# Second attention layer: output bias as a row of WO, image part added on TensorE in the head transposes, norms folded into the context columns, small steps in other slots

## The reference

```
q, k_t, v_t = heads(x @ W_q), heads(text @ W_k), heads(text @ W_v)
probs_t  = softmax(q k_t^T * scale)
text_out = probs_t v_t
k_ip, v_ip = heads(ip @ W_k_ip), heads(ip @ W_v_ip)
qsem     = l2norm(probs_t @ text)                 # per head, over 512 channels
sem      = qsem . l2norm(ip)                      # per head, 4 values
probs_ip = softmax(q k_ip^T * scale + 0.5 * sem) * spatial_mask
out = (text_out + probs_ip v_ip) @ W_out + b_out + x
```

## Time and profile before

| | |
|---|---|
| median of 3 runs | 1884.32 us |
| lowest, highest | 1880.2, 1893.85 us |
| the profiled execution | 1886.43 us |
| its span, first to last instruction | 1883.9 us |
| mean granted TensorE clock | 0.937 |
| PE busy | 1698.1 us (90%) |
| DVE busy | 1458.5 us (77%) |
| ACT busy | 1037.1 us (55%) |
| POOL busy | 876.7 us (47%) |

### The profile page before, as it was taken

The page is one execution under the profiler, slowest core; times in us unless marked ns, Lnnn a source line. Parts: engine busy times, 40 slices in busy tenths (PEclk is TensorE's granted clock), DMA queues, the critical chain, the costliest instruction groups (busy, mean ns, idle before and its releaser), DMA issues.

```text
span 1883.9 us, 42199 instructions
## 1 busy us (share of the span) xinstructions
PE 1698.1 (90%) x14344; PEld 1480.7 (79%) x14344; DVE 1458.5 (77%) x3732; ACT 1037.1 (55%) x2188; POOL 876.7 (47%) x714
## 2 busy tenths in 40 slices
PE   5999999999999998479998989898899989889885
PEld 4888888888888886368787878788788878878764
DVE  4677777777777777448988888888888888888884
ACT  3466666666666665236655555555455655545551
POOL 4223233323333321445664665566466656646563
PEclk9899999999999999679998999989898999989997
DMA  6333444434434432533233223313322331332210
GB/s 170 94 112 115 122 118 121 122 114 120 120 117 117 122 94 63 155 93 91 65 90 81 76 69 85 89 42 90 80 76 65 91 88 46 86 81 69 60 34 21
DMA packets 186492, 172.65 MB, mean 92 GB/s; under 512 B 25884, under 2 KB 186282, under 8 KB 186282
## 3 DMA queue, kind: packets, MB, share of 16 engines
q1 hardware_dynamic: 186282, 169.97, 32.1%
HBM read 110.19 MB, written 57.59 MB: 89 GB/s over the span
## 4 chain that ended last, share of the span: by engine, by line
PE 26%; DVE 15%; POOL 8%; issue 7%; ACT 2%; SPq 1%; DMA 0%; DVEq 0%; ACTq 0%; POOLq 0%
PE MISC L60 9%; PE GP L60 6%; DVE PM L1077 4%; DVE ZP L1071 4%; POOL NRM L1242 3%; PE PV L787 3%; PE NAT L736 3%; POOL ZS L1221 3%; DVE MX L1063 2%; PE TR L757 2%; PE PV L790 1%; POOL XTSL L1249 1%; ACT P L933 1%; PE MISC L886 1%; DVE NRM L1096 1%
## 5 line engine op out<-in xcount | busy, mean ns | idle before, releaser
L1221 POOL TENSOR_TENSOR ZS<-ZP 128x256 f32<-128x256 f32 x320 | 312.2, 978 | 392.5 <-DVE ZP L1071 392.1
L314 ACT ACTIVATE P<-TA 128x512 f32<-128x512 f32 x320 | 202.2, 633 | 253.5 <-DVE TA L460 252.8
L60 PE MATMUL GP<-PH,GH 128*128 128x256 f32 (+1 forms) x960 | 263.8, 302 | 50.9 <-DVE ZP L1071 50.1
L1077 DVE SCALAR_TENSOR_TENSOR PM<-P,PH 128x512 f32<-128x512 f32 x320 | 279.7, 874 | 0.0
L1071 DVE TENSOR_TENSOR ZP<-GP,PM 128x512 f32<-128x512 f32 x320 | 219.7, 687 | 70.4 <-PE GP L60 57.7
L60 PE MATMUL GP<-PH,GL 128*128 128x256 f32 (+1 forms) x960 | 254.6, 292 | 0.0
L1063 DVE TENSOR_REDUCE MX<-NAT 128x2 f32<-128x504 f32 x320 | 215.9, 676 | 40.1 <-PE NAT L736 38.0
L60 PEld LDWEIGHTS GP<-PH,GH 128*128 128x128 f32 (+1 forms) x960 | 191.9, 200 | 66.6 <-issue 41.1
L445 DVE TENSOR_REDUCE MX<-NAT 128x2 f32<-128x154 f32 x320 | 101.8, 318 | 172.2 <-PE NAT L142 170.2
L933 ACT ACTIVATE P<-TR 128x512 f32<-128x512 f32 x320 | 189.8, 593 | 63.5 <-PE TR L757 58.0
L460 DVE TENSOR_TENSOR TA<-TR,ST 128x512 f32<-128x512 f32 x320 | 219.1, 686 | 3.0 <-PE TR L162 2.8
...
## 6 DMA issues: line engine op xcount, KB each, us to landing
...
```

The lines of the kernel that those rows point to most:

```text
L60: ins = e.matmul(out, lhs, rhs, start=(n == 0), stop=(n == len(pairs) - 1))
L314: e.activation(P[:, s % NP, :], TA[:, s % 2, :], ACT.Exp, scale=SCALE).then_inc(q["exp"], 1)
L1077: e.scalar_tensor_tensor(PM[:, s % 2, :], P[:, s % NP, :], 2.0, PH[:, s % NS, :].bitcast(F32), ALU.mult, ALU.subtract).then_inc(q["pm"], 1)
L1221: e.tensor_tensor(ZS[:, s % NZ, :], ZP[:, s % 2, 0:S], ZP[:, s % 2, S:2 * S], ALU.add).then_inc(q["zs"], 1)
```

## The change

Both layers:

- The output bias is no longer added to the residual XB by POOL. WO gets it as row 111 of its third chunk, and HS a column C of ones; the chunks of the heads start at CO = (0, 112, 209).

Second layer:

- `ipm` and DVE's two additions of the image part are gone. The head transposes are now ordinary matmuls of HS with the identity, and a second matmul, VIP with PT, accumulates the image part into the same bank. `hst` is split over two slots.
- The factor 0.5 / norm of the image tokens is multiplied into the four image columns of CT by DVE (`ctn`, slot -8) before the context is split into CTSH and CTSL, so the multiplication by RN in FU goes. The norm step moves from ONCE = -12 to NORM = -34, and its input is loaded earlier.
- The norm of qsem: a product, a maximum and a scaled product become one scalar_tensor_tensor.
- The mask is applied in F1 (two scalar_tensor_tensor) and not to FM. SC is scaled by ACT and has three buffers.
- GL, HTL and the output addition stand one slot after the PE step they read, ahead of MX. Other small steps get other slots.

```diff
-    AT = dict(q=(-3, 1, 5), k=(-2, 2, 6), spill=(-1, 3, 7), x_in=-22, xts=-12, c_in=-18, cts=-6, gr=(4, 8), v=(10, 12), kbd=12, scm=14,
-              vip_in=20, vip=32, cmb=46, root=(46, 47, 48, 49), sem=(52, 53, 54), fu=55, tx=(56, 57, 58), ptt=59, ipm=61, hst=64, om=(69, 73), out=75,
-              xb_in=59, xb=63)
-    ONCE = -12
+    AT = dict(q=(-3, 1, 5), k=(-2, 2, 6), spill=(-1, 3, 7), x_in=-22, xts=-12, c_in=-18, ctn=-8, cts=-6, gr=(4, 8), gl=(5, 9), v=(10, 12), kbd=11, scm=14,
+              vip_in=34, vip=44, cmb=47, root=(47, 48, 49, 50), inv=53, f0=55, f2=57, sub=58, sum=60, f1=61, ptt=63, tx=63, hst=(67, 71),
+              htl=(68, 72), om=(75, 78), y=(76, 79), out=80, xb_in=63)
+    ONCE, NORM = -12, -34
...
-            b = due(t, AT["ipm"])
-            if b is not None:
-                for i in range(2):
-                    k, free = ring.take(("ipm", b, i), (q["hs"], 2 * b + i + 1))
...
-                    e.matmul(k[:, 0:C], PT[:, i * 128:(i + 1) * 128], VIP[:, b % 2, :], start=True, stop=True).then_inc(q["ipm"], 1)
...
+            for i, off in enumerate(AT["hst"]):
+                b = due(t, off)
+                if b is not None:
                     k, free = ring.take(("hst", b, i), (q["ht_lo"], 2 * b + i + 1))
                     e.wait_ge(*free)
                     if i == 0:
...
-                    for c, c0 in enumerate(CC):
-                        ins = e.transpose(k[0:CK, c * 128:(c + 1) * 128], HS[:, i, c0:c0 + CK], IDENT[:, :])
+                        e.wait_ge(q["tx"], b + 1)
+                        e.wait_ge(q["pt"], b + 1)
+                        e.wait_ge(q["vip"], b + 1)
+                    for c, c0 in enumerate(CO):
+                        e.matmul(k[0:CK, c * 128:(c + 1) * 128], HS[:, i, c0:c0 + CK], IDENT[:, :], start=True, stop=False)
+                        ins = e.matmul(k[0:CK, c * 128:(c + 1) * 128], VIP[:, b % 2, c0:c0 + CK], PT[:, i * 128:(i + 1) * 128], start=False, stop=True)
...
+            if t == NORM:
                 k, free = ring.take("rnm", (q["rn"], 1))
-                e.wait_ge(*free)
+                if free:
+                    e.wait_ge(*free)
                 e.wait_ge(q["once_q"], 1)
                 e.wait_ge(q["fill"], FILLS)
...
+            for n, off in enumerate(AT["gl"]):
+                b = due(t, off)
+                if b is not None:
...
+            for i, off in enumerate(AT["htl"]):
+                b = due(t, off)
+                if b is not None:
...
+            for i, off in enumerate(AT["y"]):
+                b = due(t, off)
+                if b is not None:
...
+            b = due(t, AT["inv"])
             if b is not None:
                 e.wait_ge(q["nrm"], 4 * b + 4)
...
+                e.scalar_tensor_tensor(NRM[:, 2, :, :], heads_of(b)[:, :, :, D], EPS, NRM[:, 1, :, :], ALU.mult, ALU.max).then_inc(q["cmb"], 1)
+                e.wait_ge(q["cmb"], 4 * b + 3)
                 e.reciprocal(NRM[:, 3, :, :], NRM[:, 2, :, :]).then_inc(q["cmb"], 1)
...
+            b = due(t, AT["ctn"])
+            if b is not None:
+                if b == 0:
+                    e.wait_ge(q["rn"], 3)
+                e.wait_ge(q["c_in"], 16 * (b + 1))
+                e.tensor_tensor(CT[:, :, NT:T], CT[:, :, NT:T], RN[:, 1, NI * b:NI * b + NI].unsqueeze(1).broadcast_to([128, KC, NI]),
+                                ALU.mult).then_inc(q["ctn"], 1)
+            if t == NORM:
+                e.wait_ge(q["norm"], 1)
                 e.tensor_copy(RN[:, 0, :], ring.bank["rnm"][:, 0:NIP]).then_inc(q["rn"], 1)
...
-            b = due(t, AT["xb"])
-            if b is not None:
-                e.wait_ge(q["xn_in"], 16 * (b + 1))
-                e.tensor_tensor(XB[:, :, :], XB[:, :, :], BIAS[:, :].unsqueeze(1).broadcast_to([128, 2, C]), ALU.add).then_inc(q["xb"], 1)
```

234 lines of the change are left out of this document (100 added, 134 removed).

## The result

The changed kernel takes 1777.74 us (median of 4, 1777.2 to 1785.6) against 1882.26 us before on the same chip (median of 4): a ratio of 0.9445, 95% interval 0.9395 to 0.9495. The forecast was 1806, with a range from 1784 to 1853. So the sign was right, and the time lies 6 us outside the range, on the fast side. The profiled execution took 1777.3 us, its span is 1775.2 us.

The account below looks back on a forecast made before the run. PE was taken as near its bound in the second layer, losing time to waits and half clock. 1886.4 - 78 - 4 + 1 + 4 - 2 = 1807, run median 2 lower, so 1805; stated 1806, range 1784 to 1853.

Parts of the forecast that it names:

- The bound and the slot rule: Second layer: PE near its bound; a slot costs the larger of 1.2 us + PE's extra and 1.93 + DVE's extra.
- PE's added work: Steady batch of the second layer: PE's own work rises by 0.9 us, to 54.2 us.
- The half clock: Steady batch: 1.5 us counted for one spell at 1.2 GHz in slots 15 or 16.
- The row of 13 batches: Second layer, steady batches: each gains 6.2 us, taken as 6.0, so 13 of them give 78 us.
- rival C: Second layer: no half clock at all, 57.5 us a batch or less, 1782 us in all; chance 0.10.
- Slots 3 and 4: Steady batch: slot 3 falls to 4.0 us without the bias addition, slot 4 from 6.3 to 2.3, the largest gain.
- GL's move: Slot 4: GL one slot on, counted with the absent transposes as the largest gain, 6.3 us now to 2.3.
- Slots 12 to 14: Steady batch: these slots take 2.7, 2.6 and 2.3 us, against 5.0, 3.2 and 5.2 before.
- PM in slots 3, 7 and 15: PM multiply on DVE: 1.83 us in slot 3, about 1.8 in slot 7, 2 or more in slot 15.
- The start: Second layer's start: first K 20 us late, near 812.3, but net loss only 4 us; bounds 0 and 16.
- The first layer: Bias addition leaving POOL gains 0 us there, since PE is the bound with only 1% idle.
- The end: From the last square root to the span's end: net gain 2 us, bounds 0 and 4.

## Why the prediction was right or wrong

**The bound and the slot rule: right.** The new slots, predicted and measured: 0 to 3: 2.7, 2.4, 2.3 to 2.6, 4.0 against 2.39, 2.70, 2.15, 3.65; 4 to 7: 2.3, 2.3, 2.6, 4.4 against 2.37, 2.40, 2.59, 4.53; 8 to 11: 2.3, 1.9, 3.0, 4.4 against 2.11, 1.93, 2.96, 4.53; 12 to 15: 2.7, 2.6, 2.3, 4.1 against 3.05, 2.82, 2.11, 4.35; 16 to 19: 1.9, 2.7, 3.95, 2.7 against 1.93, 2.91, 3.70, 2.83. The sum is 58.0 measured and 57.5 + 0.5 predicted. That it fits so closely is partly luck: single slots miss by up to 0.35 and cancel. Slot 3 came out 0.35 shorter, 0.26 of it by the HS multiply, which takes 0.74 up to the start of the next instruction where the forecast had 1.0; slot 12 came out 0.35 longer, since PM still takes 1.86 in it, beside two ZS in a row. (The forecast read the 2.00 of PM in slot 12 as beside CTSL; CTSL starts only in slot 14.) PE's added work was 1.0 against 0.9, though its whole, 54.2 forecast against 56.0 by busy time, was 1.8 short, as that of before was.

**The half clock: the step that failed.** The sum held 1.5 us a batch "for one half-clock spell in slots 15 or 16". Measured is one spell of 3.4 us in twelve batches, and that batch took 59.2 us against 58.0, so 0.1 us a batch. The term was 1.4 too large, 18 us over 13 batches. The row of 13 batches was missed by 18.6: 19.5 for the whole term of 1.5, 2.6 for rounding 6.2 down to 6.0 and 1.9 for slots a little shorter, less 5.4 the other way, because the mean of these batches before was 65.4 and not 65.8 (batch 14, near the end, took 60.8). The mechanism of rival C decided, with a chance of 0.10, and C's 1782 is 4 us off. The evidence that I set against C was one stretch of before, PE busy 2.44 of 3.40 us and half clock behind it. It was a stretch of a kernel that lost 5.9 us a batch in other places too, and I carried it over to one that loses 1.9. What the runs show instead, in the table: the eight kernels with 3.2 us of idle PE a batch or more had 4.6 to 10.8 us of half clock, the six with 2.8 or less had 0.3 to 2.6 (and five more that change the start of the layer, with 1.8 to 2.2, had 0 to 0.3). That is an order among the kernels of this case, and no rule: at 1.9 us of idle PE in slot 15, one kernel had 4.6 us of half clock and another, at 1.8, had 2.6; and within one kernel, batches with the same idle time have no spell, a short one or a long one. Which of the removed waits had caused which spell stays open beyond what the runs on single parts say.

The Trainium skill (TensorE: Matmul & The Clock Gate, Why this matters for your kernels) asks for no long idle gaps between bursts of matmuls, and by it C would have held; it did. But the kernel before with bias row and transposes moved cooled in slots 13 to 16 in every batch, and in ten of the twelve no single wait of PE is longer than 0.8 us; by that section alone it should not have.

**The clock was about half of the gain, and I had counted it as a remainder.** By PE's ledger 4.7 of the 7.7 us a batch are half clock and 4.0 are waits, less 1.0 of added work. The ledger charges a spell half of its length, and that is its upper end: batches with and without one, in the kernels where both occur, differ by 0.8 to 1.7 us for 3.4 and by 2.4 to 3.0 for 6.8. At these prices the 16 short and nine long spells of before are 2.9 to 4.5 us a batch (an estimate).

**Slots 3 and 4: right in mechanism, wrong in one name.** Bank and bias addition did what was said; both were shown alone. GL's move, named with the transposes as the largest gain, did nothing.

**Slots 12 to 14: partly.** They got nearly as short as predicted (8.0 against 7.6, from 13.4). DVE's removed work is 2.1 us of that and 1.4 of the batch. The rest went with what left these slots. The small steps can come back to slots 12 to 17 at no cost (0.4 us a batch is even won), but two moves stay: the subtraction out of slot 14, where it stood beside CTSL, and VIP's mask from slot 12 to 4, which the forecast's text does not name. That these two carry the rest is read from the timelines and was not run by itself. Why the kernel before keeps 5.1 us of half clock there with bank and bias cured, when the changed kernel with DVE's work back has 1.1, is not settled. With the steps spread and the mask moved no spell begins in slots 13 and 14 any more, but ten begin in 15 and 16; with the output matmuls moved alone it gets worse; the two together were not run.

**The image rows' DMA: not priced.** The forecast has no word on vip_in going from slot 0 to slot 14. In the kernel with the steps spread, leaving it cost 90 us. In the changed kernel it was moved, and what leaving it there would cost was not measured.

**PM in slots 3, 7 and 15:** 1.81, 1.80 and 2.05, as forecast. In slot 3 PM went on past the end of PARTS (1180.73), through ZS (to 1181.42), and ended at 1181.96, 0.54 behind ZS. By the Trainium skill (SBUF — State Buffer, Who interferes with whom) the second instruction is blocked until the first finishes; PM would have ended 0.55 earlier. As before the change, it stayed blocked through the POOL instruction behind as well. In slot 15 it is otherwise, and there that rule fits:

```profile
1214.34 2.41 POOL L1242 TENSOR_TENSOR CTSL<-CT,CTSH 128x1024 fp32r<-128x1024 f32 x1
1215.23 2.07 DVE L1108 SCALAR_TENSOR_TENSOR PM<-P,PH 128x512 f32<-128x512 f32 x1
1216.70 1.19 POOL L1212 TENSOR_TENSOR ZS<-ZP 128x256 f32<-128x256 f32 x1
```

PM ends 0.54 behind CTSL, and the ZS directly behind CTSL takes 1.19 instead of the 0.74 of slot 3, as if it had to let PM go first. What decides between the two orders is open.

**The start: right.** First K 19.7 us later in the layer (forecast 20; its terms add up to 811.7 and not 812.3), first ZP 3.2 later (4):

```profile
788.68 1.94 PE L61 MATMUL MISC<-XB,ONES 128*128 128x64 f32 x8 [29.27 <-DVE VIP L1056]
```

```profile
791.03 10.57 POOL L1252 TENSOR_TENSOR RN<-RN,HALF 128x64 f32<-128x64 f32 x1 [8.71 <-DVE RN L1189]
803.78 2.34 POOL L1242 TENSOR_TENSOR CTSL<-CT,CTSH 128x1024 fp32r<-128x1024 f32 x1 [2.18 <-ACT CTSH L1020]
```

But I took for given that the root has to stand there. It does not: an early root for two batches and the others batch by batch were worth 17 us.

**The first layer: 0 forecast, -5.6 measured, and mostly chance.** The period is 44.4 us in both, and 4.9 of the 5.6 us lie in the first batch. Between 60 and 85 us the clock reads 0.66 in the kernel before and 0.93 after, one spell of 17.1 us against one of 3.4:

```profile
60.00:85.00 25.00, 22.32 (x178) 18.31 (x177) 18.60 (x79) 14.19 (x33) 3.96 (x5) 0.93 0.39 117
```

Sixteen more profiles show the changed first layer: six have a spell of 3.4 us there and ten one of 13.7 or 17.1. With the long spell the second layer begins at 764.6 to 770.1, with the short one at 760.4 to 762.8. So some 5 us of the 108.7 belong to the execution and not to the change; whether the bias row makes the short spell more frequent (the old first layer showed the long one in both its profiles) stays open.

**The end:** 2.6 against 2, the four roots as long as before (7.72).
